# Context attention on one core: score maxima over pieces of 512 keys instead of 401, the left-over keys of four rows in one bank

## What is computed

```python
x = x + _L0_attn_ref(_layernorm(x, axis=-1), ...)
x = x + _L0_xattn_ref(_layernorm(x, axis=-1), ctx_768, ...)
x = x + _L0_ffn_ref(_layernorm(x, axis=-1), ...)
x = x + _L1_attn_ref(_layernorm(x, axis=-1), ...)
x = x + _L1_xattn_ref(_layernorm(x, axis=-1), ctx_768, ...)
x = x + _L1_ffn_ref(_layernorm(x, axis=-1), ...)
```

```python
attn = jnp.einsum('bhqd,bhkd->bhqk', q, k) * scale
attn = jnp.clip(attn, -CLAMP, CLAMP)
attn = jax.nn.softmax(attn, axis=-1)
x = jnp.einsum('bhqk,bhkd->bqhd', attn, v).reshape(B, Nq, Cq)
```

## Time and profile before

| | |
|---|---|
| time, median of 3 runs | 6515.49 us (6505.9 to 6515.85) |
| the profiled execution | 6520.41 us, of which span 6518.0 us |
| PE, DVE, ACT, POOL busy over the span | 82%, 72%, 46%, 32% |
| c0a, regular part | 1106 to 2284 us |
| c1a, regular part | 5041 to 6108 us |
| mean granted TensorE clock over the span | 0.887 of full speed |

### The profile page before, as it was taken

One profiled execution on the slowest core, in us unless ns is written; L12 is line 12 of the kernel. 1 busy time (PEld: TensorE's weight loads), 2 busy tenths in 40 slices (PEclk: granted clock), 3 DMA queues, 4 the chain that ended last, 5 costly groups with the idle time before them and its releaser, 6 DMA issues. The chain is left out here.

```text
span 6518.0 us, 129937 instructions
## 1 busy us (share of the span) xinstructions
PE 5340.4 (82%) x45929; PEld 2778.1 (43%) x45975; DVE 4697.5 (72%) x8463; ACT 3029.6 (46%) x4548; POOL 2056.1 (32%) x2623
## 2 busy tenths in 40 slices
PE   3588856888888849968597999998766999999669
PEld 2243343222222234424356888886434333333234
DVE  6466966999999945457656777774565999999654
ACT  0233323777777722223433444444323777777522
POOL 0201535777777730004026555550025000000000
PEclk6799977999999969989796888887977999999879
DMA  2221045222222210002344333433137222222100
GB/s 67 45 47 22 9 138 185 59 62 58 58 62 59 52 53 1 0 9 103 118 142 119 113 113 116 117 114 103 52 91 230 60 65 67 65 65 67 56 12 13
DMA packets 740085, 486.52 MB, mean 75 GB/s; under 512 B 512088, under 2 KB 673472, under 8 KB 733952
## 3 DMA queue, kind: packets, MB, share of 16 engines
q1 hardware_dynamic: 739584, 479.45, 25.9%
HBM read 281.75 MB, written 196.37 MB: 73 GB/s over the span
## 5 line engine op out<-in xcount | busy, mean ns | idle before, releaser
L1507 ACT ACTIVATE c0a_raised<-c0a_sb 128x1024 f32<-128x1024 f32 (+1 forms) x832 | 836.3, 1025 | 318.2 <-PE c0a_sb L1318 313.9
L1271 POOL TENSOR_SCALAR c0a_prob<-c0a_raised 128x1024 f32<-128x1024 f32 (+1 forms) x832 | 864.7, 1039 | 365.1 <-ACT c0a_raised L1507 333.6
L1507 ACT ACTIVATE c1a_prob<-c1a_sb 128x1024 f32<-128x1024 f32 (+1 forms) x832 | 828.4, 1029 | 201.1 <-PE c1a_sb L1318 197.3
L1395 DVE TENSOR_REDUCE c1a_pmax<-c1a_sa 128x2 f32<-128x802 f32 (+1 forms) x704 | 697.9, 991 | 64.6 <-PE c1a_sa L1286 62.1
L1395 DVE TENSOR_REDUCE c0a_pmax<-c0a_sa 128x2 f32<-128x802 f32 (+1 forms) x704 | 696.8, 990 | 55.5 <-PE c0a_sa L1286 52.3
L1286 PE MATMUL c0a_sa<-c0a_K,c0a_Q 48*128 48x401 bf16 (+1 forms) x2048 | 471.5, 350 | 182.2 <-DVE c0a_pmax L1395 105.7
L1286 PE MATMUL c1a_sa<-c1a_K,c1a_Q 48*128 48x401 bf16 (+1 forms) x2048 | 465.0, 345 | 103.8 <-DVE c1a_pmax L1395 44.5
L1337 PE MATMUL c0a_pv<-c0a_prob,c0a_V 128*9 128x256 f32 x6656 | 525.9, 387 | 4.7 <-POOL c0a_prob L1271 4.1
L1337 PE MATMUL c1a_pv<-c1a_prob,c1a_V 128*9 128x256 f32 x6656 | 517.9, 382 | 0.9 <-issue 0.5
L1286 PEld LDWEIGHTS c0a_sa<-c0a_K,c0a_Q 48*128 48x128 bf16 x2048 | 128.8, 93 | 669.9 <-DVE c0a_pmax L1395 356.8
L3110 PE MATMUL dd_lb<-dd_src 64*128 64x128 f32 (+1 forms) x3584 | 356.2, 345 | 39.0 <-DVE dd_AB L3301 15.7
(11 more groups left out here) (609 smaller groups left out, 10726.6 us busy)
## 6 DMA issues: line engine op xcount, KB each, us to landing
dd_src<-unit_in SPq DMA_DIRECT2D x32, 1024.0 KB, 7.9
k_ctx<-c0k_parts SPq DMA_DIRECT2D x16, 1200.8 KB, 5.7
c0a_K<-k_ctx SPq DMA_DIRECT2D x128, 150.1 KB
k_ctx<-c1k_parts SPq DMA_DIRECT2D x16, 1200.8 KB, 6.0
c1a_K<-k_ctx SPq DMA_DIRECT2D x128, 150.1 KB
unit_in<-ds_raw SPq DMA_DIRECT2D x32, 512.0 KB, 2.6
unit_v<-ds_vs SPq DMA_DIRECT2D x32, 512.0 KB, 2.6
unit_in<-dp_res SPq DMA_DIRECT2D x32, 512.0 KB, 3.0
```

Of the source, the lines that this page charges most:

```text
L1271: pool.tensor_scalar(prob[0:r, in_ring(v, c), :, :, :], raised[0:r, in_ring(v, c), :, :, :], 1.0, math.exp(-FLOOR), ALU.min, ALU.max).then ...
L1395: dve.tensor_reduce(pmax[:, u, :, 2 * pr + s, k], sa2[:, :, 0:w], AX.X, ALU.max).then_inc(a_reduced, 1)
L1507: act.activation(dst[0:r, in_ring(v, c), :, :, :], sb_[0:r, in_both(v, c), :, :, :], ACT.Exp).then_inc(b_exp, 1)
```

## The change

The pieces have 512 keys (`QW`), a whole bank. Three of them (`WHOLE`) cover 1536 keys, and 65 (`REST`) are left over. So there are 2 x 2 x 3 = 12 combinations of whole pieces: 9 twos and 6 ones, each with matmuls of 512 columns and reduces of 1024 or 512. The left-over keys are done in two more ones, one for each `e`: `a_rest` writes the four matmuls of 65 columns (each with another `pr` and `s`) side by side into the one bank of `sa1`, and one reduce over `p x w` with x = 4, w = 65 gives four maxima. `order` has 18 entries instead of 22 (9 twos, 8 ones, the maxima), and the maxima stand at place 7 instead of 9. `pmax` keeps four pieces a row. The number of score columns a unit (12808) and of matmuls (32) stays the same; the reduces go from 21 to 17.

```diff
--- before.py
+++ after.py
@@ -1113,8 +1113,9 @@
-    PIECES = -(-LC // 512)
-    QW = -(-LC // PIECES)
+    QW = 512
+    WHOLE = LC // QW
+    REST = LC - WHOLE * QW
...
@@ -1122,10 +1123,10 @@
-    combos = [(pr, s, k) for pr in range(2) for s in range(2) for k in range(PIECES)]
-    TWOS = 11
-    ONES = 2 * (len(combos) - TWOS)
-    M_AT = 9
+    combos = [(pr, s, k) for pr in range(2) for s in range(2) for k in range(WHOLE)]
+    TWOS = 9
+    ONES = 2 * (len(combos) - TWOS) + 2
+    M_AT = 7
...
-        pmax = st.sb("pmax", [P, 2, 2, 4, PIECES])
+        pmax = st.sb("pmax", [P, 2, 2, 4, WHOLE + 1])
...
@@ -1281,10 +1282,17 @@
                 def a_score(tile, n, v, e, combo):
                     pr, s, k = combos[combo]
-                    a, b = k * QW, min(LC, (k + 1) * QW)
                     at = slice(e * HALF, e * HALF + ROWS)
-                    return pe.matmul(tile[:, 0:b - a], Q[at, v, pr, s * P:(s + 1) * P], K[at, v, pr, a:b],
+                    return pe.matmul(tile, Q[at, v, pr, s * P:(s + 1) * P], K[at, v, pr, k * QW:(k + 1) * QW],
                                      start=True, stop=True)
+
+                def a_rest(n, v, e):
+                    at = slice(e * HALF, e * HALF + ROWS)
+                    for x in range(4):
+                        pr, s = divmod(x, 2)
+                        ins = pe.matmul(sa1[:, x * REST:(x + 1) * REST], Q[at, v, pr, s * P:(s + 1) * P],
+                                        K[at, v, pr, WHOLE * QW:LC], start=True, stop=True)
+                    return ins
...
+                    elif x < ONES - 2:
+                        ins = a_score(sa1[:, :], n, v, x % 2, TWOS + x // 2)
                     else:
-                        ins = a_score(sa1, n, v, x % 2, TWOS + x // 2)
+                        ins = a_rest(n, v, x % 2)
                     ins.then_inc(a_scored, 1)
...
@@ -1391,13 +1401,15 @@
-                        w = min(LC, (k + 1) * QW) - k * QW
-                        dve.tensor_reduce(pmax[:, u, :, 2 * pr + s, k], sa2[:, :, 0:w], AX.X, ALU.max
+                        dve.tensor_reduce(pmax[:, u, :, 2 * pr + s, k], sa2[:, :, :], AX.X, ALU.max
+                                          ).then_inc(a_reduced, 1)
+                    elif x < ONES - 2:
+                        pr, s, k = combos[TWOS + x // 2]
+                        dve.tensor_reduce(pmax[:, u, x % 2, 2 * pr + s, k:k + 1], sa1[:, :], AX.X, ALU.max
                                           ).then_inc(a_reduced, 1)
                     else:
-                        pr, s, k = combos[TWOS + x // 2]
-                        w = min(LC, (k + 1) * QW) - k * QW
-                        dve.tensor_reduce(pmax[:, u, x % 2, 2 * pr + s, k:k + 1], sa1[:, 0:w], AX.X, ALU.max
+                        dve.tensor_reduce(pmax[:, u, x % 2, :, WHOLE],
+                                          sa1[:, 0:4 * REST].rearrange("p (x w) -> p x w", x=4), AX.X, ALU.max
                                           ).then_inc(a_reduced, 1)
```

2 lines of the change are left out of this document (1 added, 1 removed).

## The result

| | before | after |
|---|---|---|
| time, median | 6515.67 us | 6537.99 us |
| span of the profiled execution | 6518.0 us | 6543.4 us |
| mean granted TensorE clock | 0.887 | 0.878 |

A forecast was written before the change was run, and what follows sets the result against it. It took the pair buffer's round, with DVE right beside it and PE's work between some pairs, as the bound. c1a 0, c0a +6 and start -1 gave 6515.5 + 5 = 6521 us, range 6478 to 6562.

The forecast's parts named there:

- the walk alone: c1a and c0a units summed pair to pair, neither rival A nor B met: 6500 to 6535 us, 45%.
- the side that had 33%: Whole kernel: slower than before by over 0.2% (13 us), given 33%.
- no change: Whole kernel: time within 0.2% (13 us) of before, given 42%.
- rival B: c0a: second cast held by a whole further POOL clip, 42 us, time 6557; 30% in any strength.
- c0a, pace at full clock: c0a units: 18.51 or 18.70 us against 18.52, taken as +0.10 a unit, +6 us over 62 units.
- The walk of c1a: c1a unit, nine steps from pair to pair: 16.94 us against 16.97 measured before, so no gain.
- rival A in full: DVE alone is the bound, so the saved reduces' fixed parts fall out: 73 us, time 6443; 8%.
- the price of the left-over group: Four 65-column matmuls on PE: taken as a full single's 0.21 us, bounds 0.11 and 0.36.
- Step 6: c1a, pair 6 to 7 to 8 to next unit, with the first left-over group: 1.75, 1.95, 1.71 us; uncertainty -0.10 to +0.15.
- step 1: c1a, pair 0 to pair 1: two chunks of one group on PE set it, 2.20 us.
- the partial form of rival A: One-group chunks at 1.05 us and left-over group at 0.11: 0.3 us a unit less, 6484 us; 17%.
- The prediction's own mark for rival B: A c0a unit above 19.1 us with casts over 0.8 us would show the forecast wrong.

The follow-up runs named there:

- the placement runs: PE's groups laid by half chunks, on the changed kernel alone, with casts as reduces, and with subtractions as reduces too: 6387.61, 6379.84 and 6361.4 us.
- fill: The changed kernel plus 19 unneeded matmuls a unit of c0a, placed where PE waits for DVE: 6499.9 us, 0.9966 of the kernel before.
- fill_other: The changed kernel plus 19 unneeded matmuls a unit of c0a, behind chunks 7 to 10 where PE has no idle time: 6668.35 us, 1.0236.
- c0a_only: The kernel before with the change in c0a alone, c1a keeping pieces of 401 keys: 6547.61 us, 1.0040 of the kernel before.

## Why the prediction came out as it did

The time, 6538, lies in the range (6478 to 6562), but outside the range of the walk alone (6500 to 6535), and on the side that had 33%. The most likely case, no change, was not what happened. That the range holds is luck in part. Its slow side was there for rival B, which didn't happen; what did happen has no term in the prediction. Its terms against the profiled execution, in us:

| | forecast | measured |
|---|---|---|
| c1a | 0 | -11 |
| c0a, pace at full clock | +6 | -6 |
| c0a, units in which the clock falls | not there | +43 |
| ends and other stages | -1 | -1 |
| span | +5 | +25 |

Two gains that it missed took 23 us off a loss that it didn't know.

**The walk of c1a was right in all steps but one.** Forecast 2.20, 1.88, 2.04, 1.71, 1.75, 1.95, 1.75, 1.95, 1.71; measured 2.18, 1.88, 2.01, 1.72, 1.74, 1.94, 1.74, 1.84, 1.71. Eight of nine are within 0.03. Its bound, DVE waiting for PE ahead of pairs where two chunks lie between, is confirmed by the placement runs. DVE's busy time fell by 61 us and brought nothing by itself, so rival A in full is wrong and the idle time did grow (though DVE waited only 252 times, four a unit, not six).

**The step that failed in c1a is the price of the left-over group.** The prediction had bounds of 0.11 and 0.36 us and took a full single's cost, 0.21. Measured against a single the group is 0.10 us shorter (0.44 against 0.54), so 0.11: the lower bound, its columns alone. The four loads of weights add nothing to that: each takes 0.09 us, and in the group shown above the second one starts at 5504.73, while the matmul of 5504.72 runs, and the four start 0.03 to 0.04 us apart instead of 0.06. Step 6 moves by -0.11. With the -0.06 of the other steps together this gives 16.77 instead of 16.94, and 62 x 0.17 = 11 us, the gain measured in c1a. A chunk of one group took 1.09 us (half of step 1), where the prediction has 1.10. This is the partial form of rival A, which was priced at 0.3 us a unit and had 17%. (Rival B's 15 us for the dearest form of this group count from 0.24 us; from the 0.21 that the walk takes they would be 19.)

**c0a at full clock was right in its unit, and not in its change.** Forecast steps 2.27, 3.12, 2.30, 1.71; measured 2.37, 3.13, 2.35, 1.70, and a unit of 18.41 to 18.53 against 18.51. The first cast ends with the second clip and takes 0.95 us, the second falls into the gap between clips (0.15 us), as laid over in the prediction. Rival B, the second cast held by the next clip, didn't happen. The unit comes out by two misses that cancel: the first four steps sum to some 0.15 us more than forecast, the other five to about as much less, most of it at the left-over group again. And the prediction didn't take this 18.51 but the middle between it and 18.70, and held it against 18.52: +0.10 us a unit. Measured, full clock against full clock, it is 18.49 against 18.59, so -0.10. The unit of before that the prediction walked is one of the short ones.

**What failed was a term that wasn't there: the clock.** The walk took all units of c0a to be at full clock, since the earlier trace rows shows 0.98. The rows had a mark of it: the measured mean was 18.72 us, the unit that was walked 18.52. A part of that difference are units of 18.6, but 10 us over the stage were fallen units, and the prediction left the gap unexplained. The change kept the pace and moved idle time of PE together, from 1.60 to 2.13 us ahead of one place. The units with a fall went from 10 to 27 and the excess from 10 to 52 us. fill shows that the excess hangs on PE's idle time there, fill_other that PE's work elsewhere doesn't prevent it. The prediction's own mark for rival B, a unit above 19.1 us with casts over 0.8 us, came true on both counts (19.27 and 0.95) with B false: the first cast was the forecast one, and the mean had another cause. A mark has to name the instruction and be read in one unit, not off a mean.

**What stays open.** Why the clock falls at the copy in some units and not in others that look the same, and so why there are 27 in one kernel and 21 in another; in most of the fallen units PE waits for 2.13 us, as in the others. That the waits decide is shown by fill and by the runs that shorten them; where between 1.05 and 1.6 us of waiting it starts isn't, as no run lies between. What pieces of 512 are worth with both kernels laid as well as they can be isn't shown either. Moving the small numbers into PSUM, another way round the holds, wasn't tried.

## What to carry to other kernels

Before you move work on the bounding pair of engines, add up where PE will wait, place by place, and look at the granted clock in single units rather than over a stage: a mean of 0.98 hid stretches at half clock, and half a microsecond more waiting in one place cost 25 us in c0a_only and 43 in after. Small DVE operations that stand on a path beside a busy POOL are cheaper as `tensor_reduce` over an axis of length one; here two such edits took 1.2% off the kernel before, over three times what the change lost. A chain held by another engine's instructions can move in whole steps of these, as here between the fifth clip and the fourth. An edit ahead of it then pays nothing or a full step, and laying it over the other engine's starts and ends tells which.

## What the runs showed of the hardware that was not expected

The granted clock falls to half, to 0.50 for 7 us in the unit shown, in a stage in which PE is busy for 86% of the time and waits nowhere for over 0.7 us in the stretch ahead. A 512-column matmul then takes 0.63 us instead of 0.39:

```profile
1308.31 0.63 PE L1286 MATMUL c0a_sa<-c0a_K,c0a_Q 48*128 48x512 bf16 x1
```

Idle matmuls where PE waited were repaid: 19 more a unit, and the kernel 0.7% faster.

Four 65-column matmuls with weights of their own start 0.03 to 0.04 us apart, so that a group costs 0.11 us of PE's time, what its 260 columns take at 2.4 GHz. And an operation on 128 x 8 numbers took 0.15, 0.29, 0.60 or 0.95 us, depending on its form and on where in a clip of 1.10 us on POOL it started.
